# TensorE's order in a gated-delta decoder layer: the out-projection in three groups instead of four, the last join beside the next turn of k, and K times state between the two turns

## What is computed

```python
mixed = silu(causal_conv4(x @ w_qkv))        # q, k: 16 heads of 128; v: 32 heads of 128
z = x @ w_z
beta, g = sigmoid(x @ w_b), -exp(A_log) * softplus(x @ w_a + dt_bias)
q, k = l2norm(q) * 128 ** -0.5, l2norm(k)    # each used by two v heads
for t in range(512):                         # state S of a head: 128 x 128
    S = S * exp(g[t])
    delta = (v[t] - k[t] @ S) * beta[t]
    S = S + outer(k[t], delta)
    o[t] = q[t] @ S
og = o * silu(z)
y = (og * rsqrt(mean(og * og) + 1e-6) * norm_w) @ w_out
x = layernorm(x + y)
```

## Time and profile before

| | |
|---|---|
| median of 3 runs | 3116.84 us (3112.36 to 3119.95) |
| span of the profiled execution (no other time is given for it) | 3112.8 us |
| TensorE matmul busy | 2954.8 us, 95% |
| VectorE busy | 2662.1 us, 86% |
| ScalarE busy | 1858.9 us, 60% |
| GpSimd busy | 642.6 us, 21% |
| mean granted TensorE clock | 0.977 of full speed |

### The profile page before, as it was taken

How to read it: one execution, slowest core, us unless ns; L and a number is a source line. 1 busy time by engine, 2 the same in 40 slices (tenths; PEclk the granted TensorE clock), 3 DMA queues, 4 the chain that set the end, 5 groups by cost and what they waited for, 6 DMA issues and landing times. The chain is left out here.

```text
span 3112.8 us, 76843 instructions
## 1 busy us (share of the span) xinstructions
PE 2954.8 (95%) x28584; PEld 2462.1 (79%) x28584; DVE 2662.1 (86%) x6061; ACT 1858.9 (60%) x5938; POOL 642.6 (21%) x911
## 2 busy tenths in 40 slices
PE   6899999999999999999999999999999999649998
PEld 3788888888888888888888888888888888536665
DVE  3788888888888989898989898888888898789984
ACT  3566666666666666666666666666666766433332
POOL 1121212121212121121212121112121211152320
PEclk9999999999999999999999999999999999859999
DMA  6423333333323333323332333333333333020000
GB/s 253 129 77 96 108 95 103 93 106 96 110 78 101 96 110 94 110 89 108 91 109 76 89 104 96 108 96 105 93 103 95 93 87 89 11 99 21 27 15 17
DMA packets 401688, 286.19 MB, mean 92 GB/s; under 512 B 231715, under 2 KB 362915, under 8 KB 383654
## 3 DMA queue, kind: packets, MB, share of 16 engines
q1 hardware_dynamic: 401318, 281.27, 29.8%
HBM read 230.49 MB, written 50.73 MB: 90 GB/s over the span
## 5 line engine op out<-in xcount | busy, mean ns | idle before, releaser
L1033 DVE SCALAR_TENSOR_TENSOR conv<-xb,convw,conv 128x512 f32<-128x512 f32 x768 | 592.9, 776 | 100.8 <-ACT conv L747 86.0
L538 PE MATMUL bank<-x_hi,w_hi 128*128 128x512 f32 x1024 | 430.6, 420 | 11.1 <-PEq L263 6.4
L538 PE MATMUL bank<-x_hi,w_lo 128*128 128x512 f32 x1024 | 404.3, 395 | 0.0
L538 PE MATMUL bank<-x_lo,w_hi 128*128 128x512 f32 x1024 | 401.3, 392 | 0.0
L741 ACT ACTIVATE xb<-bank 128x512 f32<-128x512 f32 x256 | 161.9, 632 | 303.3 <-PE bank L538 278.8
L550 PE MATMUL bank<-w_hi,x_hi 128*128 128x256 f32 x1024 | 303.1, 296 | 0.5 <-ACT conv L747 0.5
L550 PE MATMUL bank<-w_hi,x_lo 128*128 128x256 f32 x1024 | 289.8, 283 | 0.0
L550 PE MATMUL bank<-w_lo,x_hi 128*128 128x256 f32 x1024 | 289.7, 283 | 0.0
L1116 POOL TENSOR_TENSOR small<-small,half 128x4 f32<-128x4 f32 x64 | 64.5, 1008 | 1048.5 <-DVE small L864 1048.5
L1144 POOL COPY halo<-xb 128x12 f32<-128x12 f32 x256 | 99.2, 387 | 864.5 <-ACT xb L741 864.5
L538 PEld LDWEIGHTS bank<-x_hi,w_hi 128*128 128x128 f32 x1024 | 194.3, 190 | 48.3 <-issue 9.3
(11 more groups left out here) (252 smaller groups left out, 7547.6 us busy)
## 6 DMA issues: line engine op xcount, KB each, us to landing
x_hi<-x_hi_scratch SPq DMA_DIRECT2D x63, 1024.0 KB, 5.0
x_lo<-x_lo_scratch SPq DMA_DIRECT2D x63, 1024.0 KB, 8.1
E<-decay_scratch SPq DMA_DIRECT2D x64, 512.0 KB, 5.7
M_scratch<-M SPq DMA_DIRECT2D x128, 256.0 KB, 2.2
w_raw<-in_w_proj SPq DMA_DIRECT2D x64, 384.0 KB, 8.4
w_raw<-in_w_out SPq DMA_DIRECT2D x32, 256.0 KB, 7.4
Tc<-T_scratch SPq DMA_DIRECT2D x64, 128.0 KB, 2.4
xT<-in_x_chunks SPq DMA_DIRECT2D x1, 4096.0 KB, 12.5
```

What stands on the lines that cost most here:

```text
L538: mm = pe.matmul(banks[j % 2][:].rearrange("p (b t) -> p b t", b=B), lhsT=t[f"w_{p}"][:, k, j, :], rhs=t[f"x_{q}"][:, k], start=i == 0, st ...
L1033: dve.scalar_tensor_tensor(out=y3, in0=xb[:, :, i:i + C], scalar=t["convw"][:, j, i:i + 1], in1=y3, op0=ALU.mult, op1=ALU.add).then_inc(on ...
```

## The change

TensorE's order alone is changed; the instructions, their operands and their waits are the same. `turn_kq` and `read` are split in two functions each. A round's end now runs: x_part 1, the out-projection of batches 0 and 1 for both heads in one group, y_part 1, batch 2, join_a, batch 3, join_b. The next round begins: turn of k, K times state, turn of q, q times state.

```diff
--- before.py
+++ after.py
@@ -368,17 +368,16 @@
         sp.wait_ge(on["d_ends"], 16 * NS)
 
     def tensor(pe):
-        def turn_kq(s):
-            for k in range(2):
-                if k == 0:
-                    if s:
-                        pe.wait_ge(on["xf"], s)
-                    pe.wait_ge(on["silu"], 4 * s + 2)
-                elif s:
-                    pe.wait_ge(on["U_done"], s)
-                for b in range(B):
-                    mm = pe.transpose(solve_bank(k)[:, b * C:(b + 1) * C], two("kq", s)[:, b, k, :], eye)
-                mm.then_inc(on["kq_turned"], 1)
+        def turn_kq(s, k):
+            if k == 0:
+                if s:
+                    pe.wait_ge(on["xf"], s)
+                pe.wait_ge(on["silu"], 4 * s + 2)
+            elif s:
+                pe.wait_ge(on["U_done"], s)
+            for b in range(B):
+                mm = pe.transpose(solve_bank(k)[:, b * C:(b + 1) * C], two("kq", s)[:, b, k, :], eye)
+            mm.then_inc(on["kq_turned"], 1)
 
         def gram(s):
             kq = two("kq", s)
@@ -440,7 +439,7 @@
                 mm = pe.matmul(u64[lo, u], lhsT=xf[hi, u, :], rhs=U[hi, u, hi], start=True, stop=True)
             mm.then_inc(on["UF"], 1)
 
-        def read(s):
+        def read_k(s):
             if s % NC == 0:
                 return
             kq = two("kq", s)
@@ -455,6 +454,11 @@
                     b = 2 * half + i
                     mm = pe.matmul(banks[4 + half][:, i * 256:(i + 1) * 256], lhsT=kq[:, b, 0, :], rhs=St[:, b], start=True, stop=True)
                 mm.then_inc(on["KS"], 1)
+
+        def read_q(s):
+            if s % NC == 0:
+                return
+            kq = two("kq", s)
             for half in range(2):
                 pe.wait_ge(on["acc"], 4 * (s - 1) + half + 3)
                 for i in range(2):
@@ -555,9 +559,13 @@
         for r in range(-2, NS):
             state, solve, ahead = r >= 0, 0 <= r + 1 < NS, r + 2 < NS
             if solve:
-                turn_kq(r + 1)
-            if state:
-                read(r)
+                turn_kq(r + 1, 0)
+            if state:
+                read_k(r)
+            if solve:
+                turn_kq(r + 1, 1)
+            if state:
+                read_q(r)
             if ahead and r % NC == 0:
                 project(r + 2, 0)
             if solve:
@@ -594,23 +602,21 @@
             if solve:
                 x_part(r + 1, 1)
             if state:
-                out(r, 0, 0)
-                out(r, 1, 0)
+                for j in range(HJ):
+                    out(r, 0, j)
+                    out(r, 1, j)
             if solve:
                 y_part(r + 1, 1)
-            if state:
-                out(r, 0, 1)
-                out(r, 1, 1)
-            if solve:
-                join_a(r + 1)
             if state:
                 out(r, 2, 0)
                 out(r, 2, 1)
             if solve:
-                join_b(r + 1)
+                join_a(r + 1)
             if state:
                 out(r, 3, 0)
                 out(r, 3, 1)
+            if solve:
+                join_b(r + 1)
 
     def scalar(act):
         def lengths_kq(s):
```

## The result

The changed kernel takes 3186.48 us (median of 4 runs, 3179.16 to 3202.18) against 3116.01 before (4 runs): 1.0234 times as long, 95% interval 1.0212 to 1.0256. The span of the profiled execution went from 3112.8 to 3183.5, by 70.7. Forecast were 3185 and 68.4 more.

What follows compares the result with a forecast made beforehand. In rounds reading the state VectorE's chain from Y to the next Xc or R was taken to end last, elsewhere TensorE's work. 11.7 + 38.1 + 18.6 = 68.4 on 3116.8 gave 3185 us, range 3155 to 3205.

Steps and rivals of the forecast that it cites:

- Group boundaries: TensorE's out-projection at the round's end: three groups instead of four save 0.09 us a round, bounds -0.02 and 0.20.
- Head 1 ahead of y_part 1: TensorE after x_part 1: head 1 waits for its low part until 2.44, so y_part 1 starts at 4.03, +1.82.
- TensorE's path: From y_part 1 to gram: turn of k at 9.97, 0.33 later; gram at 14.78, +0.81.
- VectorE's path: Copy of Y +1.82, R at 13.43, M at 16.22: +1.19 after its 0.56 idle; +1.16 for round 33 into 34.
- From M to the next x_part 1: M's delay passes through N and the base to TensorE's y_part 0 or turn: +1.19, or +1.16 into r % 4 = 2.
- rival 1: TensorE alone sets the pace: 0.8 a boundary, 3167, or 0.33, 3138; chance 0.13 (3155 to 3170), 0.07 (down to 3130).
- Rounds without a read: Boundaries into r % 4 = 0: turn of q waits for ScalarE's copy of the last join, +0.78 each, 15 boundaries.
- Faster: All boundaries: head 1's low part and the sums come in time, 0.09 to 0.20 saved each, 3104 to 3111; chance 0.03.
- The lag not shortened at all: Reading boundaries: gram comes later too, VectorE waits again, full 1.82 each, 3216; chance 0.12 (3200 to 3225).
- A nominal change: Whole kernel: compiler or queue restores the old order; no time given; 0.02 for no change.
- the terms into 1 and 2: Reading boundaries: 1.19 each into r % 4 = 1 (with 3, 32 x 1.19 = 38.1); into 2, 16 x 1.16 = 18.6.
- the one into 3: Reading boundaries into r % 4 = 3: 1.19 each, summed with those into 1 as 32 x 1.19 = 38.1.

Runs made afterwards that it cites:

- The fitted order on VectorE: Against the changed kernel, VectorE's low part of head 1 ahead of x_part 1, copies of Tc and sums of batches 0 and 1 ahead of copying Y: ratio 1.0006.
- the four kernels of the first set: The first four follow-up kernels, run on one chip; the kernel before the change, run beside them, had a median of 3124.
- the four of the second: The next four follow-up kernels, run on one chip; the kernel before the change, run beside them, had a median of 3120.
- the two of the third: The last two follow-up kernels, run on one chip; the kernel before the change, run beside them, had a median of 3130.

## Why the prediction was right

By its own steps:

- *Group boundaries*, 0.09 (bounds -0.02 and 0.20): 0.13 where nothing else moved. The unseen passage from the last join to the turn costs what a passage costs, 1.07 from start to start (1502.77 to 1503.84). The Trainium skill's rule that a change of tiling mode drains TensorE (TensorEngine Tiling (Array Packing), section Tiling Modes) agrees as far as the passages go: the last full-array matmul steps 0.32 into the small tiles of y_part 1 instead of 0.23. That merging would save nothing was not so. A group's first matmul still steps 0.11 longer than the others, and that is now paid three times instead of four.
- *Head 1 ahead of y_part 1*, start at 2.44 and y_part 1 +1.82: 2.44 and +1.82 in every kind.
- *TensorE's path*, turn of k 9.97, gram 14.78: 9.97 and 14.80.
- *VectorE's path*, R 13.43, M 16.22, +1.19 and +1.16: 13.43, 16.24 to 16.25, +1.20 and +1.17. The cover before M, 0.56, was used up. The fitted order on VectorE shows that the late Y is the cause: filling the idle time removes the loss.
- *From M to the next x_part 1*, taken as rigid, +1.19, +1.16 and +1.19: this step holds into r % 4 = 3 alone, where the length follows N one to one; the median grew by 1.42, as N came 7.33 behind M where it took 7.14 before. Into 1 and 2 the usual rounds grew by 0.83 and 0.84. There is a second cover behind N that the forecast didn't see: N may come 0.6 later in one round than in another, and the factors start at the same time (rounds 25 and 5 in the table above). Between them stand VectorE's two products with the gate, beside GpSimd's split of the weights (a subtraction, w_lo). The split comes after a copy on ScalarE (w_hi) and moved as gram did, 28.23 to 29.06 behind x_part 1. GpSimd and VectorE before:

```profile
1488.09 3.00 POOL L1149 TENSOR_TENSOR w_lo<-w_raw,w_hi 128x512 fp32r<-128x512 f32 x2 [0.20 <-ACT w_hi L777]
```

```profile
1488.89 1.04 DVE L985 TENSOR_TENSOR O<-O,sz 128x512 f32<-128x512 f32 x1
...
1490.57 1.07 DVE L985 TENSOR_TENSOR O<-O,sz 128x512 f32<-128x512 f32 x1
```

and after:

```profile
1522.92 3.00 POOL L1155 TENSOR_TENSOR w_lo<-w_raw,w_hi 128x512 fp32r<-128x512 f32 x2 [0.24 <-ACT w_hi L783]
```

```profile
1523.95 0.81 DVE L991 TENSOR_TENSOR O<-O,sz 128x512 f32<-128x512 f32 x1
...
1525.40 1.07 DVE L991 TENSOR_TENSOR O<-O,sz 128x512 f32<-128x512 f32 x1
```

In the trace before, the 40 products with no such subtraction beside them take 0.69 each and the 56 others 0.69 to 1.75, 1.07 by the median. In the rows the first took 1.04 and takes 0.81 now: VectorE comes 1.06 later to it (29.03 to 30.09) and leaves the second 0.84 later. Into r % 4 = 3 nothing stands beside them, and there the cover is missing. So the usual rounds into 1 and 2 go by TensorE's path, rather as rival 1 had it, and reach VectorE by way of the split; once N is later than about 22.9 before and 23.6 after, VectorE's chain ends last there too, and as N moved by more than that limit, this is so in more rounds (5 of 32 before, 14 after). That the rounds don't follow N is shown by the rows; that the split is what holds them is a reading of rows, as no run moved it.
- *Rounds without a read*, +0.78 for U: +0.78 by the median, 0.98 by the sum, since 6 of 15 take 40.3 instead of 39.4 where 2 of 15 took 39.5 instead of 38.6 before. The first row here is the turn of k, the second the turn of q, on TensorE after:

```profile
1464.47 0.66 PE L379 MATMUL bank<-eye,kq 128*128 128x128 f32 x4
1465.32 0.66 PE L379 MATMUL bank<-eye,kq 128*128 128x128 f32 x4 [0.19 <-ACT U L658]
```

- *What no step had*, a slower clock: where N comes latest into r % 4 = 1, TensorE waits for R and then for Xc. That is so in two rounds before (1 and 53) and in five after (1, 5, 21, 37, 49). Round 21:

```profile
1030.29 0.63 PE L513 MATMUL bank<-eye,R 128*128 128x128 f32 x4 [1.06 <-ACT R L719]
...
1032.12 1.06 PE L424 MATMUL bank<-Xc,Uc 32*32 32x32 f32 x64 [1.21 <-DVE Xc L951]
```

Then the granted clock was 0.5 for 3.4 us, 1.2 GHz instead of 2.4, and from y_part 0 to x_part 1 it took 3.42 (1032.12 to 1035.54) where round 32 took 2.03. The clock fell so in both of the two rounds before and in four of the five after (in round 5 it stayed). Rounds with the wait of 1.21 alone kept the full clock. In round 21 the low clock is thus worth about 1.4 of the 2.5 us by which the round is over the median.

The rivals: TensorE as the sole bound (3167 or 3138): excluded as a whole, since the rows of Xc and R did not shrink and into r % 4 = 3 the length follows N; but its 0.8 a boundary is what the usual rounds of the other three kinds paid. Faster: VectorE would have needed 1.5 us to spare. The lag not shortened at all (3216): M started at 16.24, not 16.86. A nominal change: the timeline has the new order.

The size came out within 1.5 us partly by luck. Against the medians the terms into 1 and 2 are 7.5 us too high, the one into 3 is 3.5 too low, and the rounds over their median (a late N, a low clock), for which it had no term, brought another 7.

## What to carry to other kernels

Before moving work on the busiest engine, find who waits for what stands behind it, and put the delay of that piece, not the saved boundary, against the slack of the waiting engine: here 0.13 us saved a round stood against 1.82 of delay and 0.56 of slack before M. An order on one engine is only as good as the order on its partner: the same TensorE order cost 2.3% or nothing, depending on whether VectorE had its sums to do while Y was late. And test a chain that is called rigid on the trace itself, before any run: take two rounds in which its input comes at different times and see whether its end differs. Here it did in one kind of round of three, and that would have named the second cover.

## What the runs showed of the hardware beyond what was expected

The time of N behind M, a DMA to DRAM and back, is not the same in kernels that issue the same transfers, and it went with the chip rather than with the kernel. Medians over 62 rounds: 7.40 to 7.45 in the four kernels of the first set, 7.22 to 7.32 in the four of the second, 7.35 and 7.40 in the two of the third, each set on one chip; 7.18 before the change and 7.25 after. It is one execution of each, and the kernel before wasn't traced on those chips. In rounds whose length follows N, 0.2 to 0.3 us each, 3 to 5 us over those into r % 4 = 3, are beyond what an argument from order alone can tell.
